# Score masks of the maxima on VectorE, local products in sets, own keys ahead of near keys, local mask last, values 17 columns apart

## The reference

```python
# layer A ("local"), 16 heads of 16: each token sees 44 earlier positions
_OFFSETS = list(range(41)) + [128, 96, 384]
k_mod = k_g * (1.0 + scale_embed)                      # one vector of 16 per offset
scores = einsum('bhtd,bhtjd->bhtj', q, k_mod) / 4 + pos_bias
scores = where(idx >= 0, scores, finfo.min)            # no position before the first
out = einsum('bhtj,bhtjd->bhtd', softmax(scores), v_g)
# layer B ("causal"), 16 heads of 16
scores = where(tril, einsum('bhqd,bhkd->bhqk', Q, K) / 4, -inf)
out = einsum('bhqk,bhkd->bhqd', softmax(scores), V)
# after each layer: x = x + experts(layernorm(x)), top 2 of 8 experts ("F")
```

## Time and profile before

| | us |
|---|---|
| median of 3 runs | 1962.25 (1960.55 to 1966.32) |
| the profiled execution, its own time | 1972.26 |
| its span, first to last instruction | 1970.2 |
| PE busy, share | 1745.7, 89% |
| DVE busy, share | 1297.8, 66% |
| ACT busy, share | 804.7, 41% |
| mean granted TensorE clock | 0.949 of 2.4 GHz |

### The profile page before, as it was taken

One profiled execution on the slowest core, in us unless ns is written; L12 is line 12 of the kernel. 1 busy time (PEld: TensorE's weight loads), 2 busy tenths in 40 slices (PEclk: granted clock), 3 DMA queues, 4 the chain that ended last, 5 costly groups with the idle time before them and its releaser, 6 DMA issues.

```text
span 1970.2 us, 29536 instructions
## 1 busy us (share of the span) xinstructions
PE 1745.7 (89%) x11263; PEld 918.3 (47%) x11312; DVE 1297.8 (66%) x3090; ACT 804.7 (41%) x1473; POOL 119.0 (6%) x155
## 2 busy tenths in 40 slices
PE   5588888899999899998999999998999899998976
PEld 2163454345453555436453455435554345454443
DVE  6939764785659756686659757696566964745433
ACT  1123425234453445434462434533454253452623
POOL 1010110001000100002000010001000010000000
PEclk9779988999999999999999999999999999998989
DMA  8220250014200250005200240003400023104000
GB/s 287 90 73 23 98 172 3 23 70 144 58 24 23 105 165 3 24 22 204 67 23 23 81 167 23 24 23 138 132 24 1 23 105 127 50 2 129 3 11 11
DMA packets 47842, 137.91 MB, mean 70 GB/s; under 512 B 6184, under 2 KB 18856, under 8 KB 42920
## 3 DMA queue, kind: packets, MB, share of 16 engines
q1 hardware_dynamic: 47704, 136.02, 21.1%
HBM read 80.79 MB, written 46.04 MB: 64 GB/s over the span
## 4 chain that ended last, share of the span: by engine, by line
PE 59%; DVE 28%; issue 5%; ACT 3%; DMA 3%; POOL 0%; SPq 0%; POOLq 0%; DVEq 0%; ACTq 0%
PE bank L1435 22%; DVE arena_AB L1216 15%; PE bank L1703 6%; PE bank L1718 5%; DVE arena_AB L1272 4%; PE bank L1606 4%; PE bank L1625 3%; PE bank L1523 3%; PE bank L1537 2%; PE bank L1590 2%; PE bank L1558 2%; PE bank L1456 2%; PE bank L1443 1%; PE bank L1608 1%; DMA arena_AB<-stacks 1%
## 5 line engine op out<-in xcount | busy, mean ns | idle before, releaser
L1216 DVE TENSOR_TENSOR arena_AB<-qT,kT 128x512 f32<-128x512 f32 x704 | 428.4, 683 | 8.6 <-ACT kT L971 7.6
L1435 PE MATMUL bank<-arena_F,kept 128*128 128x512 f32 (+1 forms) x544 | 265.3, 615 | 15.8 <-ACT cont_hi L1059 4.2
L1523 PE MATMUL bank<-arena_AB,slot_w 128*32 128x512 f32 x1408 | 212.4, 643 | 54.9 <-DVE arena_AB L1216 52.9
L1272 DVE TENSOR_REDUCE arena_AB<-bank 128x1 f32<-128x512 f32 (+3 forms) x512 | 214.5, 481 | 67.6 <-PE bank L1592 66.0
L1069 ACT ACTIVATE arena_F<-bank,kept 128x512 f32<-128x512 f32 x256 | 169.0, 691 | 152.0 <-PE bank L1435 149.6
L1034 ACT ACTIVATE arena_AB<-bank 128x512 f32<-128x512 f32 (+1 forms) x352 | 178.7, 577 | 105.9 <-PE bank L1608 105.6
L1435 PEld LDWEIGHTS bank<-arena_F,kept 128*128 128x128 f32 (+1 forms) x544 | 93.6, 190 | 124.0 <-issue 99.2
L1590 PE MATMUL bank<-arena_AB 96*128 96x512 bf16 (+3 forms) x512 | 132.9, 317 | 10.0 <-ACT arena_F L1069 3.3
L1606 PE MATMUL bank<-arena_AB 99*128 99x256 bf16 (+3 forms) x512 | 127.3, 305 | 3.2 <-DMA arena_AB<-maxima 3.0
L1703 PE MATMUL bank<-arena_F,kept 128*64 128x512 f32 x512 | 126.0, 613 | 3.0 <-issue 1.9
L1435 PE MATMUL bank<-xnT,kept 128*128 128x512 f32 x256 | 125.7, 630 | 2.1 <-ACT xnT L953 1.7
(11 more groups left out here) (192 smaller groups left out, 2493.7 us busy)
## 6 DMA issues: line engine op xcount, KB each, us to landing
arena_AB<-band SPq DMA_DIRECT2D x32, 1344.0 KB, 6.3
arena_AB<-stacks SPq DMA_DIRECT2D x64, 384.0 KB, 8.4
stacks<-arena_AB SPq DMA_DIRECT2D x48, 256.0 KB, 2.9
band<-arena_AB SPq DMA_DIRECT2D x32, 328.0 KB, 2.2
stacks<-xnT SPq DMA_DIRECT2D x32, 256.0 KB, 2.6
band<-kT SPq DMA_DIRECT2D x4, 1352.0 KB, 21.8
v<-V SPq DMA_DIRECT2D x8, 576.0 KB
stacks<-xn SPq DMA_DIRECT2D x16, 256.0 KB, 3.1
```

The costliest lines, as they stand in the source:

```text
L1216: nc.vector.tensor_tensor(prod[n % RD], qT[:, hf, :], kT[:, hf, at:at + T], ALU.mult).then_inc(sem["A"]["prod_made"], 1)
L1272: ins = nc.vector.tensor_reduce(neg_max[:, n, i:i + 1], ps[:, at:at + (i + 1) * P], AX, ALU.max, negate=True)
L1435: ins = nc.tensor.matmul(out(ps), w, x, start=n == 0, stop=n == len(pairs) - 1)
L1523: ins = nc.tensor.matmul(ps[HS * col:HS * (col + 1), :], slot_w[:, slot(n), :], prod[n % RD], start=False, stop=r == 3, skip_group_check=True)
```

## The change

1. B: the mask matmul of each raw piece goes. VectorE's reduction becomes a fused instruction that adds a mask from SBUF (zeros ahead of the triangle, so `causal` is 512 wide), negates, writes the result back into the bank and keeps the minimum. The planner's TensorE costs for `S` become smaller, its VectorE costs stay.
2. A, products: one VectorE instruction for a set, over overlapping slices of `kT`; the offsets 96, 128 and 384 each have one of their own. The ring is 4 sets (`RQ`), and a set signals once.
3. A: the local mask is added last, over as many columns as the largest offset of the group needs: 40, 24 or 384.
4. A, output: all 16 own products, then all 16 near ones.
5. Values 17 columns apart: a head's 32 weight columns now reach into the next head's values, and those 15 output rows are not used.

```diff
-PACK_S = [... ("ahead", T), ("causal", P),
+PACK_S = [... ("ahead", T), ("causal", T),
...
-RD = 18
+RQ = 4
...
+def runs(q):
+    near = [n for n in SETS[q] if slot(n) < NEAR]
+    return [near] + [[n] for n in SETS[q] if slot(n) >= NEAR]
...
-        p.put(("prod", q), ("DVE", 0.605 * len(of), *needs), ("PE", 1.3 if r == 0 else 0.95))
+        p.put(("prod", q), ("DVE", 0.08 * len(runs(q)) + 0.534 * len(of), *needs), ("PE", 0.95 if r < 3 else 1.15 if g == NG - 1 else 1.0))
...
-            p.put(("oT", i), ("PE", 2.0, *needs), ("ACT", 0.55))
+            p.put(("oT", i), ("PE", 1.4, *needs), ("ACT", 0.55))
...
-        p.put(("S", h, n), ("PE", (0.3, 0.45, 0.25)[n], ("stack", h // 4, "DMA")), ("DVE", (0.62, 0.8, 0.36)[n]))
+        p.put(("S", h, n), ("PE", (0.22, 0.23, 0.12)[n], ("stack", h // 4, "DMA")), ("DVE", (0.62, 0.8, 0.36)[n]))
...
-        V = sb("V", [P, TT, H, HS])
+        V = sb("V", [P, TT, VW])
...
-                        for n in SETS[i]:
-                            at = PAD - SLOTS[slot(n)]
-                            if n >= RD:
-                                dve.wait_ge(*product_used(u, n - RD))
-                            nc.vector.tensor_tensor(prod[n % RD], qT[:, hf, :], kT[:, hf, at:at + T], ALU.mult
-                                                    ).then_inc(sem["A"]["prod_made"], 1)
+                        if i >= RQ:
+                            dve.wait_ge(*products_used(u, i - RQ))
+                        for run in runs(i):
+                            col, at, c = PRODUCTS[run[0]][2], PAD - SLOTS[slot(run[0])], len(run)
+                            k = kT[:, hf, at:at + T]
+                            k = bass.AP(k.tensor, k.offset, [k.ap[0], [4, c], [1, T]])
+                            ins = nc.vector.tensor_tensor(prod[i % RQ][:, col:col + c, :],
+                                                          qT[:, hf, :].unsqueeze(1).broadcast_to([P, c, T]), k, ALU.mult)
+                        ins.then_inc(sem["A"]["prod_made"], 1)
...
-                            ins = nc.vector.tensor_reduce(neg_max[:, n, i:i + 1], ps[:, at:at + (i + 1) * P], AX,
-                                                          ALU.max, negate=True)
+                            s = ps[:, at:at + (i + 1) * P]
+                            ins = nc.vector.tensor_tensor_reduce(
+                                out=s, in0=s, in1=causal[:, (TT - 1 - i) * P:T], scale=-1.0, scalar=BIG, op0=ALU.add,
+                                op1=ALU.min, accum_out=neg_max[:, n, i:i + 1])
...
-                        if r == 0:
-                            rows = GROUP_J[g] * HPT
-                            nc.tensor.matmul(ps[0:rows, :], is_slot[:, g * P:g * P + rows], ahead[:], start=True,
-                                             stop=False, skip_group_check=True)
...
+                            rows, cut = GROUP_J[g] * HPT, max(SLOTS[slot(n)] for k in SETS[i - 3:i + 1] for n in k)
+                            nc.tensor.matmul(ps[0:rows, 0:cut], is_slot[:, g * P:g * P + rows], ahead[:, 0:cut],
+                                             start=False, stop=True, skip_group_check=True).then_inc(full_, 1)
...
                         for g in range(4):
                             for col in range(4):
                                 ins = nc.tensor.matmul(ps[HS * col:HS * (col + 1), g * P:(g + 1) * P],
-                                                       V[:, i, 4 * g + col, :], ptA[:, 4 * g + col, :],
-                                                       start=True, stop=True)
-                            for col in range(4 if i > 0 else 0):
+                                                       V[:, i, columns_of(4 * g + col)], ptA[:, 4 * g + col, :],
+                                                       start=g == 0, stop=True, skip_group_check=True)
+                        for g in range(4 if i > 0 else 0):
+                            for col in range(4):
...
-                        nc.tensor.matmul(ps[:, at:at + (i + 1) * P], q_st[0:K, h, i * P:(i + 1) * P],
-                                         k_st[0:K, h, 0:(i + 1) * P], start=True, stop=False, skip_group_check=True)
-                        ins = nc.tensor.matmul(ps[:, at + i * P:at + (i + 1) * P], ident_b[:], causal[:],
-                                               start=False, stop=True, skip_group_check=True)
+                        ins = nc.tensor.matmul(ps[:, at:at + (i + 1) * P], q_st[0:K, h, i * P:(i + 1) * P],
+                                               k_st[0:K, h, 0:(i + 1) * P], start=True, stop=True)
```

More of the change, by code:

```diff
@@ L13 @@
 HS = 32
+HV = HD + 1
+VW = H * HV + HS - HV
 HPT = P // HD
@@ L26 @@
 NEG = -1.0e30
+BIG = 3.0e38
 EPS = 1e-5
@@ L144, in local_phases @@
         needs = [("qk", hf, "ACT"), ("qk", KD + hf, "ACT")]
-        needs.extend(("prod", k, "PE") for k in range(q) if of[-1] - RD in SETS[k])
-        p.put(("prod", q), ("DVE", 0.605 * len(of), *needs), ("PE", 1.3 if r == 0 else 0.95))
+        if q >= RQ:
+            needs.append(("prod", q - RQ, "PE"))
+        p.put(("prod", q), ("DVE", 0.08 * len(runs(q)) + 0.534 * len(of), *needs), ("PE", 0.95 if r < 3 else 1.15 if g == NG - 1 else 1.0))
         if r == 3:
@@ L609, in build @@
         xnT_ab = sb("xnT", [P, KD, T])
-        prod = [part(T, at=r * T) for r in range(10)]
+        prod = [part(4 * T, at=4 * r * T).rearrange("p (c t) -> p c t", c=4) for r in range(2)]
+        taken["AB"] = 10 * T
         band = part(2 * BW * H, at=0).rearrange("p (r s h) -> p r s h", r=2, s=BW)
@@ L613, in build @@
         sT = part(2 * NG * T).rearrange("p (g t) -> p g t", g=2 * NG)
-        prod.extend(part(T, at=taken["AB"] if r == 0 else None) for r in range(8))
-        assert len(prod) == RD
+        prod.extend(part(4 * T).rearrange("p (c t) -> p c t", c=4) for _ in range(2))
+        assert len(prod) == RQ
         p_nat = part(2 * J * H, at=sT_at + 2 * NG * T).rearrange("p (r j h) -> p r j h", r=2, j=J)
@@ L733, in covered, with products_used @@
             return [x for x in latest(u, others) if FILLS[u, x][0] != FILLS[u, name][0]]
[L735 to L739, removed]
+        def products_used(u, q):
+            if q % 4 == 3:
+                return bank_full(u, ("sT", q // 4))
+            return nth(u, "prod_used", q - q // 4 + 1)
         def step_done(u, n):
@@ L744, in step_done, with heads, columns_of @@
             return bank_full(u, ("oT", g)) if k == TT - 1 else nth(u, "pv_done", 3 * g + k + 1)
+        def heads(v):
+            return v[:, :, 0:H * HV].rearrange("p i (h d) -> p i h d", h=H)
+        def columns_of(h):
+            return slice(h * HV, h * HV + HS)
         def rows_of(dram, batch):
@@ L1543, in local_attention @@
                         ps, full_ = place(u, name, full)
-                        nc.tensor.matmul(ps[:, 0:P], ident_b[:], causal[:], start=True, stop=True)
+                        nc.tensor.matmul(ps[:, 0:P], ident_b[:], causal[:, 0:P], start=True, stop=True)
                         for h in range(8 * q, 8 * q + 8):
```

57 lines of the change are left out of this document (29 added, 28 removed).

## The result

The changed kernel takes 1933.08 us (median of 4 runs, 1931.68 to 1937.36), beside 1963.17 for the kernel before on the same chip (1960.55 to 1966.32). The ratio is 0.985, with a 95% interval from 0.9828 to 0.9872: 30 us less, where 31 were forecast. The profiled execution took 1931.68 us with a span of 1929.6, so here the profile is 1 us under its median, while that of before was 9 us above its own.

A forecast was written before the change was run, and what follows sets the result against it. The prediction took TensorE and VectorE to bound the kernel by turns. Its terms, -22 - 16 - 14 - 2 + 20 + 2 + 1 = -31 us, took 1962 to 1931 us, with a range of 1893 to 1958.

The forecast's parts named there:

- Products in sets: A's products on VectorE: 464 fewer instructions at 0.067 us each, 31 us of work, -22 us of time.
- The 70% from the chain's shares: Products on VectorE: 301 of their 428.4 busy us stand in the chain, so 70% of the saving counts.
- Own keys, then near keys: A's output on TensorE: ending the alternation saves 0.65 us a tile, over 24 tiles -16 us, bounds -10 and -21.
- Masks off TensorE: B's raw scores: 512 masks at 0.06 us, of which 232 count, -14 us, bounds -7 and -31.
- maxima with mask: B's maxima on VectorE: 0.09 us more a piece, 220 pieces in the chain, +20 us, bounds +11 and +70.
- The slower rival: First ten heads of each B call: reading and writing the same bank halves the rate, about 2045 us; chance 0.14.
- the gain get eaten: B's maxima: the second instruction costs its whole 0.156 us, +50 instead of +20, about 1961 us; chance 0.15.
- all of TensorE's cuts turn into time: Whole kernel: the new order fills VectorE-bound stretches with F, -65 us, about 1897 us; chance 0.13.
- The clock: First raw scores: the forecast is wrong if an emptier TensorE falls to half its clock more often; no size given.
- The ring: Products in A: TensorE may fall three sets, 6.6 us, behind, and the shorter ring costs 0.
- `cont_lo` first: B calls: it stands ahead of the first maxima, some 0.6 us behind the first raw score, +2 us, bounds 0 and +5.
- What would show it: Signs in the profile: TensorE's busy time about 50 us lower, idle about 20 higher, 32 maxima at 0.49 us each.

The follow-up runs named there:

- masks_on_both: The changed kernel with the 512 mask matmuls put back on TensorE while VectorE still adds its own mask: ratio 0.9948 to the kernel before.
- ring5: The changed kernel with a ring of five sets of products instead of four: ratio 0.9817 to the kernel before.
- all_undone_old_costs: The changed kernel with VectorE masks, separated own and near keys, and product sets undone, its order planned with the earlier costs: ratio 1.0013 to the kernel before.
- old_costs: The changed kernel with all its parts, its order planned with the earlier costs for products, raw scores and A's output: ratio 0.9848 to the kernel before.

## Why the prediction was right, term by term

**Sum.** -31 forecast, -30 measured. That the middle was hit so closely is partly luck. Priced in the old order, where they add up, the parts are: sets -16 (-22 taken out last) where -22 was forecast, own and near keys -18 where it was -16, the mask part +2 where it was +6, and all the rest +3 where it was +1. Misses of 2 to 6 us cancel, and the intervals of single steps are 3 to 4 us wide to each side, so they can't be told from noise one by one.

**Products in sets, -22.** The price of an instruction, 0.067 us, held: busy time 397.7 where 397 was forecast, 429.3 with single products. Overlapping slices cost nothing extra (4 x 0.535 + 0.067 = 2.21 us forecast for a set of four, and four such sets take 8.90 us in the row below, less 0.08 of overhang: 2.205 each). Of the 31 us, 16 to 22 counted in the old order and 29 in the new. The 70% from the chain's shares is the upper of the old order's two values.

```profile
607.50 8.90 DVE L1237 TENSOR_TENSOR arena_AB<-qT,kT 128x2048 f32<-128x2048 f32 x4
```

**Own keys, then near keys, -16.** A tile saves 2.28 - 1.43 = 0.85 us (0.65 taken, 0.86 the bound): 24 x 0.85 = 20. Measured: 18 in the old order, 21 in the new. Within the intervals all of it is on the path, as assumed. What was a little too dear is the near part of a tile: 0.55 us of it was left in the forecast, and 663.44 - 663.02 = 0.42 us are left in the trace.

**Masks off TensorE -14, maxima with mask +20.** Both terms were mis-sized, both too slow, and together they gave +6 where the runs gave -10 (new order) and +2 (old order). The next two sizes are from the new order, so the order's misfit may be in them; no run tells the two apart in the old order. A piece costs 0.046 us more, not 0.09, and it lies under the lower bound of 0.06: the second instruction isn't paced at 0.06 behind the first, it runs beside the next piece. The addition is 9 us of time and not 20, the masks are 19 and not 14. The step that failed for the addition is the one that priced the second instruction by the small ones of the earlier trace rows. The slower rival, by which writing into the bank read halves the rate, fell: 0.046 us, where 0.17 was the point of decision. Nor did the gain get eaten, or all of TensorE's cuts turn into time: 1933 against their 1961 and 1897.

**The clock.** The prediction named it last, among what would make it wrong, and gave it no price. It happened: 68 us at the lower level against 19 to 22 of the kernel before in the eight windows of first raw scores. The 19 us of masks_on_both are what was left of the cut with this loss in it.

**The ring, 0.** Wrong in kind: "VectorE waits 8.6 us in all ahead of products now, 7.6 of it for keys, so 0" reads a wait of before as if it could not grow. There are 21.6 us of waits for a free set where the row of before has none, and ring5 won back some 6 us of time with half of them. VectorE waiting in the product stretch was one of the prediction's own signs of being wrong; it came true and cost little. The order is not the main cause: in the old order the changed kernel still waits 18.8 us.

```profile
L1237 DVE TENSOR_TENSOR arena_AB<-qT,kT 128x2048 f32<-128x2048 f32 (+3 forms) x240 | 397.0, 1716 | 27.7 <-PE bank L1543 15.6 <-ACT kT L990 8.0 <-PE bank L1550 3.2
```

With single products and the old order (all_undone_old_costs) the ring of four sets has 9.8 us of them, so about half comes with the ring and its one signal a set, and half with faster products. Nor is it much shorter in products: 4 sets of 4 are 16, where there were 18 slots. But a set of the last group of offsets has only three products and still takes a whole place, so the ring holds 12 there. That is where most of the waits are: 1024-wide instructions occur in these sets alone, and 16.9 of the 21.6 us stand in front of them (the change, by form).

```profile
L1237 DVE TENSOR_TENSOR arena_AB<-qT,kT 128x1024 f32<-128x1024 f32 x48 | 58.7, 1222 | 17.3 <-PE bank L1543 12.8 <-PE bank L1550 4.1
```

**`cont_lo` first, +2.** Its wait grew from 64.0 to 87.6 us. In old_costs, where `cont_lo` stands behind seven maxima, it waits 59.7 us, and the maxima wait 60.4 us instead of 45.7. So half of the added wait was moved from the maxima, and the time of the two kernels is the same: no run shows a cost of +2. The local mask, the values 17 apart and the setup are in the 0.0013 of all_undone_old_costs and were not told apart; a kernel with the local mask 512 wide was not run. The larger setup pack took 9.8 us to land instead of 7.9.

**What would show it.** TensorE's busy time lower by 59.5 (50 forecast), its idle time higher by 19 (20 forecast), A's tile 1.43 us (1.4 to 1.9), eight heads of maxima 32 x 0.448 = 14.3 us (15.7). Four raw scores in a row at full clock take 0.71 us to the modelled end of the last. A 512-wide one is shown as 0.38 us where the next matmul starts 0.22 us behind it (742.47 and 742.69 us in the same trace), so some 0.16 of it is overhang, and 0.55 is left (0.56 forecast):

```profile
748.24 0.71 PE L1617 MATMUL bank<-arena_AB 96*128 96x512 bf16 x4
```

## What to carry to other kernels

Price a part in an order of work that suits the kernel without it as well. Undone one at a time in an order planned for the fast version, three parts seemed to be worth 60 us, and undone together there 54; in the old order the three together were worth 32, and the whole change brings 30. When a part takes matmuls away from TensorE in a stretch where it already waits for another engine, read the granted clock there: the work saved may come back as work done at half speed. And a row that shows no wait for a buffer says nothing of a ring that is freed in larger pieces; count what it holds where the pieces are smallest, and what the reader does between two uses.

## What the runs showed of the hardware

VectorE's combined addition and minimum with an accumulated result is two instructions in the trace, and the read of the accumulator (140 ns) overlaps the next piece; the pair costs 0.046 us more than a plain reduction, on average over pieces of 128 to 512 columns. It writes in place into the bank that it reads at 1.04 ns a column (0.65 us from a 512-wide piece to the next, 0.25 us from a 128-wide one).

The matmul of a 128 x 128 mask behind each raw score costs 0.06 us of TensorE's time at full clock and went with a granted clock of 1.00 at the first raw scores of the second to sixth B call in 32 of 35 cases (7 profiles of 5 calls). Without it, the clock was 1.00 there in 4 of 35, and mostly 0.83 to 0.94. In the first B call it was 0.67 to 0.76 with the mask matmuls and 0.50 to 0.59 without.
